# A 16-image attention kernel on one core: the pixel-major copy of the normalized image leaves TensorE, and every engine's order is rewritten

## The reference, cut to what matters

```python
# block 0: depthwise 3x3 conv (3 outputs per channel), 1x1 up, gelu, 1x1 down, residual
hid = gelu(einsum(perceived(x), w_up1) + b_up1);  h = x + einsum(hid, w_up2) + b_up2
# 3x3 windowed local attention on h, and residual
y = h + local_attn(h, w_qkv, b_qkv)
# block 1: group norm over (pixels, 16 channels of a group), 8 groups
xn = (y - mean) * rsqrt(var + 1e-3) * gamma + beta
# attention of all 1024 pixels over all 1024 pixels, and residual
q = xn @ Wq + bq;  k = xn @ Wk + bk;  v = xn @ Wv + bv
out = xn + (softmax(q @ k.T * C**-0.5) @ v) @ Wp + bp
```

## Time and profile before

| what | value |
|---|---|
| median of 3 runs | 1008.86 us (1008.59 to 1011.76) |
| the profiled execution's own time | 1009.14 us |
| its span, first to last instruction | 1007.4 us |
| PE busy | 959.1 us, 95% |
| PEld busy | 847.1 us, 84% |
| DVE busy | 830.8 us, 82% |
| ACT busy | 611.7 us, 61% |
| POOL busy | 363.6 us, 36% |
| mean granted TensorE clock | 0.985 |
| bytes moved by DMA | 152.79 MB in 171648 packets |

### The profile page before, as it was taken

How to read it: one execution, slowest core, us unless ns; L and a number is a source line. 1 busy time by engine, 2 the same in 40 slices (tenths; PEclk the granted TensorE clock), 3 DMA queues, 4 the chain that set the end, 5 groups by cost and what they waited for, 6 DMA issues and landing times.

```text
span 1007.4 us, 18575 instructions
## 1 busy us (share of the span) xinstructions
PE 959.1 (95%) x5556; PEld 847.1 (84%) x5556; DVE 830.8 (82%) x1596; ACT 611.7 (61%) x1250; POOL 363.6 (36%) x334
## 2 busy tenths in 40 slices
PE   4888999999999999999999999999999999999985
PEld 3876978889898988989898898989889898888774
DVE  6857888988787998888899898879979888898862
ACT  2575755757476575747667574666757466576531
POOL 4526045260433526142352615235261524431110
PEclk9997999999999999999999999999999999999998
DMA  5100753637457363745737373663737366346683
GB/s 96 22 2 1 210 157 116 188 105 218 128 175 197 117 187 104 224 120 182 193 115 187 112 220 116 194 180 115 187 120 213 115 198 177 124 159 202 200 285 108
DMA packets 171648, 152.79 MB, mean 152 GB/s; under 512 B 71648, under 2 KB 155104, under 8 KB 171616
## 3 DMA queue, kind: packets, MB, share of 16 engines
q1 hardware_dynamic: 170768, 152.00, 51.9%
q10 hardware_dynamic: 848, 0.39, 0.2%
HBM read 76.87 MB, written 75.50 MB: 151 GB/s over the span
## 4 chain that ended last, share of the span: by engine, by line
PE 69%; issue 6%; DVE 5%; DMA 2%; POOL 2%; ACT 1%; SPq 0%; DVEq 0%; ACTq 0%; POOLq 0%
PE work L681 18%; PE work L521 8%; PE work L523 8%; PE work L522 8%; PE work L594 3%; PE work L616 3%; PE ps_s L521 2%; PE ps_s L522 2%; PE ps_s L523 2%; PE ps_t L521 2%; PE work L657 2%; PE ps_t L522 2%; PE ps_t L523 2%; DVE et L1828 2%; PE work L580 2%
## 5 line engine op out<-in xcount | busy, mean ns | idle before, releaser
L681 PE MATMUL work<-et,vv_t 128*128 128x256 f32 x1024 | 237.2, 385 | 6.8 <-DVE et L1828 5.7
L681 PEld LDWEIGHTS work<-et,vv_t 128*128 128x128 f32 x1024 | 192.5, 191 | 38.3 <-DVE et L1828 11.3
L1399 POOL TENSOR_TENSOR g_lo<-u,g_hi 128x512 fp32r<-128x512 f32 x60 | 76.7, 1279 | 317.9 <-ACT g_hi L978 317.9
L521 PE MATMUL work<-t_lo,wc_hi 128*128 128x256 f32 x576 | 170.2, 295 | 6.0 <-POOL t_lo L1399 6.0
L1828 DVE STREAM_TRANSPOSE et<-e_by_keys 128x1024 f32<-128x1024 f32 x128 | 158.2, 1237 | 20.4 <-DMA e_by_keys<-e_blocks 19.6
L523 PE MATMUL work<-t_hi,wc_hi 128*128 128x256 f32 x576 | 163.6, 284 | 0.0
L522 PE MATMUL work<-t_hi,wc_lo 128*128 128x256 f32 x576 | 162.6, 282 | 0.0
L521 PEld LDWEIGHTS work<-t_lo,wc_hi 128*128 128x128 f32 x576 | 110.6, 192 | 7.7 <-POOL t_lo L1399 6.9
L522 PEld LDWEIGHTS work<-t_hi,wc_lo 128*128 128x128 f32 x576 | 110.7, 192 | 0.8
L523 PEld LDWEIGHTS work<-t_hi,wc_hi 128*128 128x128 f32 x576 | 109.9, 191 | 0.0
L1060 ACT ACTIVATE e<-ps_t,nm 128x1024 f32<-128x1024 f32 x64 | 71.2, 1113 | 46.2 <-DVE et L1828 42.2
(11 more groups left out here) (175 smaller groups left out, 2330.5 us busy)
## 6 DMA issues: line engine op xcount, KB each, us to landing
e_blocks<-e SPq DMA_DIRECT2D x128, 512.0 KB, 3.3
e_by_keys<-e_blocks SPq DMA_DIRECT2D x128, 512.0 KB, 4.7
x_in<-in_x SPq DMA_DIRECT2D x64, 128.0 KB, 5.1
out<-r_tok SPq DMA_DIRECT2D x32, 256.0 KB, 3.4
w_up_t<-in_L_conv_w_up SPq DMA_DIRECT2D x1, 384.0 KB, 3.8
const<-in_const ACTq DMA_DIRECT2D x1, 166.0 KB, 5.0
y<-in_L_conv_w_up ACTq DMA_DIRECT2D x1, 128.0 KB, 4.7
y<-in_L_conv_w_qkv SPq DMA_DIRECT2D x1, 128.0 KB, 4.6
```

Of the source, the lines that this page charges most:

```text
L521: te.matmul(dst, wh, xl, start=first, stop=False)
L681: mm = te.matmul(bank("pv", j, n)[:, 0:256], vv_t[:, kt, :], et[:, kt, pixels_], start=kt == 0, stop=kt == TILES - 1)
L1399: return pool.tensor_tensor(dst, full, hi, ALU.subtract)
```

## The change

**What it does.** (1) `vv` on TensorE and `vv_half` on ACT are gone. In their place SP stores `y` (as `xn`) to DRAM, `xn_out`, one transfer of 512 KB. `xn_in` loads it back in four transfers of 128 KB in pieces of 128 bytes, and `xn_turn` on DVE transposes 128x1024 in 32x32 blocks into `vv_t`. The next image's `y_half` waits for the store in place of `vv`. (2) The four small group-norm operations become `tensor_scalar` with per-partition scalars. (3) The last two tiles of the last image don't go through DRAM: `probs_t` on TensorE transposes them into the PSUM bank of the scores, and `et_copy` on ACT copies them to `et`. `exp` waits differ for these tiles. (4) The lists of all engines and the bank plans are reordered.

```diff
-            def vv(n, half):
-                te.wait_ge(*xn_ready.after(n, half))
-                te.wait_ge(*bank_free("vv", half, n))
-                for t in range(4):
-                    pix = slice((4 * half + t) * 128, (4 * half + t + 1) * 128)
-                    mm = te.transpose(bank("vv", half, n)[:, t * 128:(t + 1) * 128], y[:, pix], ident)
-                mm.then_inc(pe["vv"].handle, 1)
-            def vv_half(n, k):
...
-                act.activation(vv_t[:, 4 * k:4 * k + 4, :], bank("vv", k, n)[:, :].rearrange("p (t c) -> p t c", t=4),
-                               ACT.Copy).then_inc(vv_ready.handle, 1)
+            def xn_out(n):
+                sp.wait_ge(*xn_ready.after(n, 1))
+                sp.dma_start(xn_rows, y[:, :]).then_inc(xn_stored.handle, 16)
+            def xn_in(n):
+                sp.wait_ge(*xn_stored.after(n, 0))
+                blocks = xn_rows.rearrange("(j q) (b a i) -> a j (q b) i", j=32, q=4, b=TILES, a=4, i=32)
+                for part in range(4):
+                    sp.dma_start(xn_by_pixels[32 * part:32 * (part + 1), :].rearrange("j (k i) -> j k i", i=32), blocks[part]) \
+                      .then_inc(xn_moved.handle, 16)
+            def xn_turn(n):
+                dve.wait_ge(*xn_moved.after(n, 0))
+                dve.wait_ge(*pe["pv"].after(n - 1, 3))
+                dve.wait_ge(*r_tok_ready.after(n - 1, 1))
+                dve.transpose(vv_t[:, :, :].rearrange("p b (j q) -> p q b j", q=4),
+                              xn_by_pixels[:, :].rearrange("p (q b j) -> p q b j", q=4, b=TILES)).then_inc(vv_ready.handle, 1)
```

```diff
-                dve.scalar_tensor_tensor(moments[:, 1:2], moments[:, 0:1], moments[:, 0:1], moments[:, 1:2],
-                                         ALU.mult, ALU.add).then_inc(gn_step.handle, 1)
+                dve.tensor_scalar(moments[:, 1:2], moments[:, 0:1], moments[:, 0:1], moments[:, 1:2],
+                                  ALU.mult, ALU.add).then_inc(gn_step.handle, 1)
...
-                dve.tensor_tensor(gn_a, gamma, rstd, ALU.mult).then_inc(gn_step.handle, 1)
+                dve.tensor_scalar(gn_a, gamma, rstd, 1.0, ALU.mult, ALU.mult).then_inc(gn_step.handle, 1)
...
-                dve.scalar_tensor_tensor(gn_nb, g_mom[:, 0:1], gn_a, beta, ALU.mult, ALU.subtract) \
+                dve.tensor_scalar(gn_nb, g_mom[:, 0:1], gn_a, beta, ALU.mult, ALU.subtract) \
```

```diff
+        def by_pe(n, t):
+            return is_last(n) and t >= TILES - 2
+            def probs_t(n, t):
+                te.wait_ge(*e_ready.after(n, t))
+                for kt in range(TILES):
+                    mm = te.transpose(score_tile(n, t)[:, kt * 128:(kt + 1) * 128], e[t % 2][:, kt * 128:(kt + 1) * 128], ident)
+                mm.then_inc(pe["t"].handle, 1)
-                act.wait_ge(*et_ready.after(n, t - 3 if t < TILES - 1 else t - 2))
+                act.wait_ge(*et_ready.after(n, t - 2 if t == TILES - 1 or by_pe(n, t + 1) else t - 3))
+            def et_copy(n, t):
+                act.wait_ge(pe["t"].handle, t - 5)
+                act.wait_ge(*et_ready.after(n, t - 1))
+                act.activation(et[:, :, t * 128:(t + 1) * 128].rearrange("p b (q j) -> p b q j", q=4),
+                               score_tile(n, t)[:, :].rearrange("p (b j q) -> p b q j", b=TILES, q=4), ACT.Copy) \
+                   .then_inc(et_ready.handle, 1)
```

More of the change, by code:

```diff
@@ L443, in turn_program @@
                 move_out(a, 4)
+                xn_in(a)
                 move_in(a, 3)
@@ L468, in drain_program @@
                 move_out(B - 3, 6)
+                xn_out(B - 2)
                 move_in(B - 3, 5)
+                xn_in(B - 2)
+                store(B - 3, 0)
                 move_out(B - 3, 7)
@@ L472, in drain_program @@
                 move_in(B - 3, 7)
-                store(B - 3, 0)
                 move_out(B - 2, 0)
@@ L491, in drain_program @@
                 move_out(B - 1, 0)
+                store(B - 2, 0)
+                xn_in(B - 1)
                 move_out(B - 1, 1)
                 move_in(B - 1, 0)
-                store(B - 2, 0)
                 move_out(B - 1, 2)
@@ L710, in fill_program @@
                 fold(1)
+                make_weights()
                 conv(0, 0)
@@ L715, in fill_program @@
                 conv(0, 4)
-                make_weights()
                 conv(0, 5)
@@ L1186, in fill_program @@
                 k_half(1, 1)
+                t_hi_part(2, 0)
+                q_half(1, 1)
+                local_exp(1, 0)
+                exp(0, 0)
+                local_scale(1, 0)
+                exp(0, 1)
+                local_exp(1, 1)
                 qq_hi_half(0, 1)
-                t_hi_part(2, 0)
-                vv_half(0, 1)
+                take(2, 0, 1)
+                pt_pair(1, 0)
+                exp(0, 2)
                 t_hi_part(2, 1)
-                local_exp(1, 0)
@@ L1268, in turn_program @@
                 gelu(c, 1)
+                gelu(c, 2)
                 g_hi_part(c, 0)
-                gelu(c, 2)
                 gelu(c, 3)
@@ L2066, in drain_program @@
                 combine_own(B - 1, 3, 6.0, 1, 5)
+                halo_turn(B - 2, 3)
                 end_row(B - 1, 4, 0, 6)
-                halo_turn(B - 2, 3)
                 end_row(B - 1, 5, 3, 7)
+                y_half(B - 2, 0)
+                et_turn(B - 3, 2)
+                y_half(B - 2, 1)
+                row_max(B - 3, 5)
+                channel_moments(B - 2)
                 et_turn(B - 3, 3)
-                row_max(B - 3, 6)
-                y_half(B - 2, 0)
-                y_half(B - 2, 1)
@@ L2111, in drain_program @@
+                row_max(B - 2, 4)
+                output(B - 3, 1)
+                xn_turn(B - 2)
                 row_max(B - 2, 5)
                 halo_turn(B - 1, 3)
+                et_turn(B - 2, 2)
                 y_half(B - 1, 0)
                 row_max(B - 2, 6)
+                et_turn(B - 2, 3)
                 y_half(B - 1, 1)
                 channel_moments(B - 1)
-                et_turn(B - 2, 3)
                 group_variance(B - 1)
```

701 lines of the change are left out of this document (342 added, 359 removed), and 54 rows, old and new, of tables (BANK_PLAN, DRAIN_PLAN, FILL_PLAN).

## The result

| | median | runs | profiled execution, span |
|---|---|---|---|
| before, four runs | 1008.73 us | 1005.40 to 1011.76 | 1009.14, 1007.4 |
| after | 1038.72 us | 1035.91 to 1040.51 | 1040.51, 1038.7 |

The ratio is 1.029, 95% interval 1.025 to 1.033: slower by 30 us, where 20 us less were forecast. Rival B had given 1028.

A forecast was written before the change was run, and what follows sets the result against it. TensorE's stream of work was taken to bound the 58.7 us turn. Savings of 10.7 us (turns), 6.2 (fill) and 3.5 (tail), 20.4 together, from 1008.86 gave 988.5 us; likeliest range 984 to 994 (0.64), wider range 981 to 999.

The forecast's parts named there:

- Rival B: In the turns, the copy's issue and landing stay whole on VectorE's path: TensorE waits 3.3 us a turn, 1028 us; chance 0.05.
- So I expect 0 to 0.5 us of new wait in a turn at this place: Behind y_half, at kk(b, 0): 0.2 us of slack against a 2 us slip, group norm giving back; turn left at -0.89.
- The slip: In the turn, y_half(b, 0) delayed by the wait for the copy's loads and its transpose: 4.5 us, cut to some 2.
- Part 1: TensorE loses eight transposes per image: 0.89 us a turn, 10.7 us in 12 turns, 1.8 in the fill, 0.9 in the drain.
- Part 3: Group norm's two slow steps fall to 0.15 us: 1 us off VectorE's chain a turn, 0.5 us in the fill.
- Nothing in TensorE's turns: Group norm with scalars shortens VectorE's chain but gains TensorE nothing in the turns.
- part 5: Tail: 1.8 us from the last tiles, 0.9 from image 14's transposes, 0.8 from earlier group norm: 3.5 us.
- Part 4: Fill: make_weights and biases moved ahead, two late steps set earlier, plus transposes and group norm: 6.2 us, bounds 1 and 9.
- 0 if the convolutions start later by what `make_weights` takes: Fill: lower bound of the 2 us counted for moving make_weights and biases ahead; the upper was 3.6.
- the 3.63 us: Fill: ScalarE's first gelu was this late, for biases, which waited on make_weights set between convolutions.
- the Trainium skill's rule that stood beside B: 128x128 transposes belong on TensorE if PSUM can take the result; by it, moving them is a loss, 1028 us.

The follow-up runs named there:

- e1: Kernel after with the normalized image's store and four loads moved to the end of the turn before, first and last images adapted: 1010.0 us.
- e5: Kernel after with only load_x(d), the image's four loads, moved back behind the load of tile 4 in the turn: 1021.6 us.
- e6: Kernel after with VectorE's transpose of the normalized image writing its runs with stride 1, not 4; part of the output uses permuted pixels: 1031.3 us.
- e10: Kernel before's orders with group norm's edit, copy through DRAM stored a turn ahead in channel order, transpose late behind the last halo transpose: 1043.0 us.
- e3: Kernel before with only the four small group-norm steps as tensor_scalar: 998.7 us.
- e8: Kernel before with only TensorE's make_weights moved ahead of the first convolution in the fill: 1018.1 us.
- e2: Kernel after's order with the pixel-major copy back on TensorE and ScalarE, without its store, loads and VectorE transpose: 1024.4 us.
- e4: Kernel before with only the last two tiles of the last image transposed by TensorE and copied by ScalarE: 1007.8 us.
- e13: e1 with the fill's first 45 us in the old order, v_half(c, 0) ahead of the tiles' transposes, last image's loads ahead of its first tile's store: 1014.4 us.
- e15: e13 with v_half(c, 0) put back behind the tiles' transposes, as in the kernel after: 1003.1 us.
- old-order runs: Four runs with the kernel before's orders, adapted in one, and the copy through DRAM, stored and loaded a turn ahead: 1036.1 to 1048.6 us.
- e9: Kernel after with store and loads a turn ahead, one channel-permuted store, make_weights back behind the fifth convolution, last image's loads ahead of its first tile's store: 1025.4 us.

## Why the prediction was wrong, step by step

**The step that failed: "So I expect 0 to 0.5 us of new wait in a turn at this place".** It followed the late `xn_turn` to `y_half` and `kk(b, 0)` and left out its first reader, `values(a, 0)`, which reads `vv_t`. In the kernel before, `vv_t` was written in the turn before, so this input was never late; in the new order it is written just ahead of its use. TensorE waited there in eight of the nine turns, 8.0 us in all of its 15.1 idle. e1 shows that the late arrival as a whole is worth 28.8 us. `kk(b, 0)`, which the working watched, isn't among the waits of that view. The wait at `values(a, 0)` isn't all of it either: e5 has none and a turn 0.67 us longer than e1's, while VectorE still waits 1 us a turn. Only 0.2 us a turn of that difference is a wait of TensorE that the view names, for ScalarE's `a_all`.

**The slip was mis-sized too.** "Some 2 us" measured 2.95 of wait and 2.04 of transpose in the turn shown, 5.0. Issue took 5.74 and not 4.23, at a DMA share of 0.90, the transpose 2.04 and not 1.24 (e6: the write stride). `load_x(d)` had been moved in front of this string of transfers, and the working did not count its 5.1 us there; e5 gives 17.2 us of the 30 for that alone. Nor did `exp(a, 3)` ahead of `take` bring the transfers 2.5 us sooner. The store of tile 4 stands at 488.35, and TensorE started `scores(a, 1)` of that turn at 469.72: 18.6 us, against 19.5 before (532.46 and 512.92), so 0.9 sooner. The store of tile 3 is issued at 485.75, right when `load_x(d)` is through with its issue.

**Part 1, right in size, wrong in use.** The eight transposes had stood in TensorE's stream for 1.0 us a turn (510.23 to 511.24), against 0.89 forecast. Their time comes out only where something else covers what they covered: e10's wait before the projection. And e1, with nearly no wait left, has a turn of 58.17 against e3's 58.02 with the transposes.

**Part 3, the small steps were right** (0.21 and 0.27 us for 0.15 forecast), and half was given back by the large ones, as the text allowed. "Nothing in TensorE's turns" was wrong: e3 gained 0.59 a turn, because the wait of 0.31 before `values(a, 2)` was the end of VectorE's chain through group norm to that tile. The prediction had it in hand and booked it only in the upper bound. The Trainium skill's statement on GpSimd and VectorE (GPSIMD Engine Reference, 8. Key points) had two halves: two inputs in SBUF, or a 2-port mode. The large `tensor_scalar`, 544 to 1014 ns, agrees with the second. The small ones didn't wait; in which mode they ran no run shows. Had they waited, the 0.8 us of part 5 would have gone too, and not the 0.5 alone that the working names.

**Part 4 had the wrong sign.** Minus 6.2 was forecast, 7.8 more came. `make_weights` in front cost 8 us in e8; in the changed kernel the other moves hold that to 3.6 at the first convolution. The bound "0 if the convolutions start later by what `make_weights` takes" left out what it waits for. And there was nearly nothing to win. The first gelu also needs the end of VectorE's chain, `end_row`, which in the kernel before ends at 43.61, and it started at 43.80:

```profile
42.08 0.28 DVE L1672 TENSOR_TENSOR bp_row<-ps_s,bp_row 128x128 f32<-128x128 f32 x1
42.28 0.14 DVE L1673 TENSOR_TENSOR cols<-ps_s,cols 128x2 f32<-128x2 f32 x1
42.34 1.27 DVE L1707 TENSOR_TENSOR u<-u,work 128x512 f32<-128x512 f32 x2
```

VectorE didn't stand idle before `biases` (the first two rows). It had come to them only then, by its order, and they took 0.3 us. So the 3.63 us were VectorE's chain and no wait for `make_weights`. In the kernel after the biases are done at 32.07, and the gelu waits for `end_row` until 45.19. The second `group_moments` is 3.4 us late (132.0 and 135.4), and the other 4.4 of the 7.8 come in the first turn. e1, whose copy is early there, has a first turn of 62.7 us like the kernel before (62.9), against 67.3. But e2 has 67.0 without any copy through DRAM, which no run explains.

**Part 5.** Minus 3.5 was forecast, the rest is 3 us longer. The last tiles gave 0.7 us and not 3.2 (e4), within the error. The loads in front of the last image's tiles, charged with 1.4, cost 0.9 to 2.6 with the order of the stores (e13 and e15 against e1).

**The rivals.** B named the mechanism, issue and landing whole on VectorE's path with the DMA engines full where the loads are issued (0.90), and its time of 1028 lay 11 us below the median. Its price of 3.3 us of wait a turn was more than the 1.72 + 0.89 = 2.6 that the turn lost; fill and tail, where it kept the gains, were what it had too low. It got 0.05 for the DMA share of 0.55. That is a turn's mean; the window of the place itself showed 0.89 in the kernel before, and neither says what stands in front in a queue that works in order. Whether the Trainium skill's rule that stood beside B (VectorE: DVE Perf Modes, Rules for kernel authors) holds as such is not shown: e1 has the copy off TensorE and a turn of 58.17, and e3 with the transposes on TensorE 58.02.

**The signs named in advance.** Wrong: the turn of 57.8 (60.33), no wait above 1 us before `xn_turn` (2.1 in the mean, 29.3 over 14), the first gelu at 40.5 (45.19). Right: no `vv`, the small steps, VectorE's idle time, the last store some 7 us behind the start of `values(3)`. Both ways of being wrong that it named came: a new wait in each turn before `values`, but for the copy and not for a tile, and a fill whose waits moved.

**What stays open.** Why the moved copy's turn of 58.17 isn't 57.1 (e3's less the transposes): e1's view shows 0.3 us of idle time a turn, and the other 0.7 lies in no wait that it names. No run took it apart, nor the first turn and the drain of the old-order runs, nor e2's first turn. Whether the full DMA engines or the place in the queue made the copy late was not separated.

## What to carry to other kernels

When a buffer's writer is moved, list every reader of it and its distance from the new writer, before following the chain that the writer delays. When work is taken off the bounding engine, look what other engine's step ran beside it: that step is waited for now. A transfer that nothing hurries belongs where its queue is idle, here a turn ahead. Take the DMA share from the few microseconds where the transfer is issued, not from the turn: 0.9 hid in a mean of 0.55. Before an engine's late step is put down to the input that came last, look whether the engine that makes this input stood idle or was busy with its chain. And a wait of 0.3 us in each turn is worth following to its origin: the edit there took 6 us off the eleven intervals, of its ten in all.

## What the runs showed of the hardware

- The 32x32-block transpose of 128x1024 takes 1.24 us when it writes runs with stride 1 and 2.04 when its writes are 4 elements apart (e6).
- A store of 512 KB whose pattern begins with a dimension of 4 landed after 11 us at a DMA share of 0.22, and after 4.2 with 128 rows outermost; among the other transfers of a turn it was 9 to 10 and 6.1 (e9, e1).
- The issue of four transfers of 128 KB took 5.74 us of SP's time in a stretch with a DMA share of 0.90, and 3.15 in one with 0.46 (after, e1).
- A small `tensor_scalar` on VectorE (0.21 to 0.27 us) didn't wait for a running GpSimd instruction where `tensor_tensor` and `scalar_tensor_tensor` of one number took 1.2 us, to that instruction's end; the 128x512 `tensor_scalar` behind them then took 1.01 for 0.54 (before, e3).
- Behind 7.5 and 2.0 us of idle time TensorE's granted clock was 0.50, the lower level of 1.2 GHz, from 25 to 35 us, and twelve small matmuls took 2.56 us for 1.40 at clock 1.00 (e8, before).
